# Round two of a graph propagation in 128 PSUM columns, and three steps moved off VectorE

## The chip, the cores and the metric
The kernel runs on one core of one Trainium2 chip. Its metric is the device time in microseconds (us) of one execution. A core has TensorE (matmuls; PE in the profile, its weight loads are the row PEld), VectorE (DVE), ScalarE (ACT), GpSimd (POOL) and SyncE (SP, which here issues all the transfers). Matmuls write into PSUM; the other memory, SBUF, has 128 partitions.

## What is computed
The input x has 4096 rows of 128 features, adj is a 4096 x 4096 matrix of zeros and ones. Cut to what matters:

```
xh   = layernorm(x)
U    = softmax over edges of leaky_relu(xh @ a1 + (xh @ a2).T)    # 4096 x 4096
feat = shrink(c1 * xh + U @ xh - rowsum * xh)
pu   = U @ feat
x1   = x + mix(feat, pu, h0, rowsum)
z, xBC, dt = split(layernorm(x1) @ W_in)                          # Mamba-2 block
xBC  = silu(causal conv of 4 taps (xBC)); xs, B, C = split(xBC)
dt   = softplus(dt + dt_bias); dA = dt * -exp(A_log)              # 4 heads
y    = within-chunk part (exp of segment sums of dA) + state part + D * xs
out  = x1 + rmsnorm(y * silu(z)) @ W_out @ W_lin + b_lin
```

U is never built. exp(leaky_relu(f1 + f2)) is one of two products of a row weight and a column weight, depending on the sign of f1 + f2. So each edge has a code, and from a block of codes two masks of zeros and ones are made: maskA for positive logits, maskC for the others. U times something is maskA times Y of side 0 plus maskC times Y of side 1, where Y holds the column-weighted features.

## The kernel before
The 4096 rows are 32 tiles of 128 (NT = 32). Masks are in fp32r, a type of 4 bytes that TensorE multiplies in one pass, where plain fp32 takes two instructions; Y keeps each feature as a high part (rounded to fp32r) and a low part (the rest), `Y[:, jt, side, part, :]`. A mask is the stationary operand of its matmul; the moving operand is both parts of Y side by side. In round one these are 2 x 130 columns (features and two extra columns), in round two 2 x 128 = 256. The result therefore stands in PSUM as two halves (high and low) which VectorE adds later.

Round one: adj is loaded, transposed on TensorE (L1223), coded by VectorE (L683) and stored to DRAM as int8 codes; masks of 128x1024 are made by ScalarE (maskA, L1053) and VectorE (maskC, L691); `products` (L1273) multiplies them. Between the rounds Y is made anew from feat, in four quarters of 8 column tiles (y_second, L670).

Round two runs in slots, one tile in each (`slot` in each engine's block, ordered by `schedule`, L235). In slot s TensorE works on the products of tile s, four blocks (block(0) to block(3)) of 8 maskA and 8 maskC matmuls, and between the blocks on the Mamba-2 steps of the tiles s-1 to s-4, one stage behind another (`ok[0]` to `ok[4]` say which exist). Five slots after the last products drain the stages. The order on each engine is written out by hand; engines wait for each other by semaphores only. Masks rotate through 4 buffers, so that a new mask waits for the matmuls of the block four before it.

What the change touches, with the lines of the kernel before:
- TensorE: L1283 and L1293 (products), L1421 (the segment sums: `after`, a triangular matrix of ones, times dam, 4 heads x 128), L1442 (B times C, which needs C on partitions 0 to 63, `cT`). Both rounds go through `products`; XC = 130 columns in round one, F = 128 in round two.
- VectorE: L845 (weighted sum of accC and the scaled accA, both halves at once, into `part`), L862 (adds the two halves), L867 (x1), L912 (`normalise2`, the second layernorm), L985 and L986 (last product of the convolution's silu into xbc; L986 does it again for C, to the lower partitions).
- ScalarE: L1072 (read_acc, scales accA), L1152 (xn2T, copy of the transposed tile, which releases L1386), L1160 to L1205.
- GpSimd: L562, L563 (rstd of the second layernorm), L573 (dam = upto times dA, 128x512), L581 to L592.
- dam and `after` are plain fp32. dA, 4 numbers for each partition, stands in `tiny`.

Of the kernel before, what the change touches and what calls it, by code (L numbers as in the profile page):

```python
# [36 lines left out]
def gnn_ffn_kernel(nc, x, adj, h0, a, temp, W_in, conv_w, conv_b, dt_bias, A_log, D, norm_w, W_out, W_lin, b_lin, out):  # L37
# [20 lines left out]
    with ExitStack() as ctx:  # L58
# [9 lines left out]
        adj_in = sb("adj_in", [P, 4, IT, JH * P])  # L68
        edges = sb("edges", [P, 4, IT, 2 * P], BF16)
        code = sb("code", [P, 2, IT, NT * P], I8)  # L70
# [54 lines left out]
        class Space:  # L125
# [43 lines left out]
        upto = rows_space.take(P)  # L169
        after = rows_space.take(P)  # L170

# [29 lines left out]
        junk = y_space.take(DI)  # L201
        sum2 = y_space.take(2 * F)
        tiny = rows_space.take(16, 8)
# [13 lines left out]
            mix_ready xdt_ready  ps_ready y_read yg_ready st_done skip_ready yT_ready ssq_ready rs_ready  # L217
            exp_done out_done zcopy""".split()
        S = {n: sem(n) for n in names}
# [156 lines left out]
        def _(pool):  # L376
# [179 lines left out]
            def slot(s_, k, now, then, ok):  # L556
                if ok[0]:

                    kt = (k - 1) % SLOTS
                    wait(pool, "ln_done", s_)  # L560
                    wait(pool, "xn2_ready", s_ - 1)
                    link(g.tensor_tensor(tiny[:, 1, 0:1], tiny[:, 0, 1:2], consts[:, 2, 0:1], ALU.add))  # L562
                    g.tensor_tensor(tiny[:, 1, 1:2], tiny[:, 1, 0:1], consts[:, 0, 0:1], ALU.pow).then_inc(S["rstd2"], 1)  # L563

                    wait(pool, "out_done", s_ - 4)
                    g.tensor_tensor(x1b[:, kt], x1[:, kt % 2], b_row, ALU.add).then_inc(S["x1b_done"], 1)
                if now:
                    base_of(s_, k)
                if ok[1]:

                    wait(pool, "dt_ready", s_ - 1)
                    wait(pool, "p_cum", s_ - 2)
                    g.tensor_tensor(dam, upto.unsqueeze(1).broadcast_to([P, NH, P]),  # L573
                                    tiny[:, 2 + k % 2, NH:2 * NH].unsqueeze(2).broadcast_to([P, NH, P]), ALU.mult).then_inc(S["dam_ready"], 1)
                if ok[2]:

                    kc = (k - 3) % 2
                    wait(pool, "xl_ready", s_ - 2)
                    wait(pool, "p_s", s_ - 3)
                    dtc = tiny[:, 2 + kc, 0:NH]  # L580
                    link(g.tensor_tensor(heads(xdt, HD), heads(xl[:, 0:DI], HD), dtc.unsqueeze(2).broadcast_to([P, NH, HD]), ALU.mult))  # L581
                    wait(pool, "exp_done", s_ - 2)
                    g.tensor_tensor(heads(xdtd, HD), heads(xdt, HD), expD[:, :, P - 1:P].broadcast_to([P, NH, HD]), ALU.mult).then_inc(S["xdt_ready"], 1)
                    wait(pool, "st_done", s_ - 3)
                    g.tensor_tensor(heads(pstate[0:DS], HD), heads(state[0:DS, kc], HD),
                                    tiny[0:DS, 4 + kc, NH:2 * NH].unsqueeze(2).broadcast_to([DS, NH, HD]), ALU.mult).then_inc(S["ps_ready"], 1)
                if ok[3]:

                    wait(pool, "ssq_ready", s_ - 3)
                    wait(pool, "out_done", s_ - 4)  # L590
                    link(g.tensor_tensor(tiny[:, 6, 0:1], tiny[:, 6, 1:2], consts[:, 3, 0:1], ALU.add))
                    g.tensor_tensor(tiny[:, 6, 2:3], tiny[:, 6, 0:1], consts[:, 0, 0:1], ALU.pow).then_inc(S["rs_ready"], 1)  # L592
                end_chain()
# [6 lines left out]
        def _(dve):  # L600
# [223 lines left out]
            def slot(s_, k, now, then, ok):  # L824
# [6 lines left out]
                kt = (k - 1) % 2  # L831
                part = sum2.rearrange("p (a b) -> p a b", a=2)
                if ok[4]:
# [29 lines left out]
                if ok[0]:  # L863

                    dve.wait_ge(S["vch"], halves)
                    wait(dve, "x1b_done", T - 1)
                    v.scalar_tensor_tensor(out=x1[:, kt], in0=part[:, 0], scalar=row_out[:, bass.ds(row, 1), 0:1].rearrange("p a b -> p (a b)"), in1=base[:, kt],  # L867
                                           op0=ALU.mult, op1=ALU.add).then_inc(S["x1_done"], 1)
# [38 lines left out]
                def normalise2():  # L907

                    if ok[0]:
                        dve.wait_ge(S["rstd2"], s_)  # L910
                        wait(dve, "p_xT", s_ - 2)
                        v.tensor_scalar(xn2[:, kt], x1[:, kt], tiny[:, 0, 0:1], tiny[:, 1, 1:2], ALU.subtract, ALU.mult).then_inc(S["xn2_ready"], 1)  # L912

# [18 lines left out]
                if ok[1]:  # L932
# [25 lines left out]
                    last = step(v.tensor_tensor(p, horner[:, 2, :, 5], si, ALU.mult))  # L958
                    normalise2()
                    y_state()  # L960
# [7 lines left out]
                else:  # L968
                    normalise2()
                    y_state()  # L970
# [7 lines left out]
                if ok[1]:  # L978
# [5 lines left out]
                    wait(dve, "p_y", s_ - 3)  # L984
                    v.scalar_tensor_tensor(out=xbc[:, k2], in0=gate_t, scalar=1.0, in1=conv, op0=ALU.add, op1=ALU.mult)  # L985
                    v.scalar_tensor_tensor(out=cT[0:DS, k2], in0=gate_t[DS:P, CB - 1], scalar=1.0, in1=conv[DS:P, CB - 1], op0=ALU.add,  # L986
                                           op1=ALU.mult).then_inc(S["conv_ready"], 1)
                mask(3)
# [6 lines left out]
        def _(act):  # L995
# [66 lines left out]
            def read_acc(T, k, cols, round_two=0):  # L1062
# [7 lines left out]
                w = roww[:, bass.ds(row, 1), 0:1].rearrange("p a b -> p (a b)")  # L1070
                src = accA[k][:, 0:2 * cols].rearrange("p (a b) -> p a b", a=2)
                s.mul(acc_s[:, k, :, 0:cols], src, w).then_inc(S["acc_read"], 1)  # L1072

# [66 lines left out]
            def slot(s_, k, now, then, ok):  # L1140
# [71 lines left out]
        def _(pe):  # L1212
# [60 lines left out]
            def products(n, k, b, ch, cols, y=None, between=None):  # L1273
# [78 lines left out]
            def slot(s_, k, now, then, ok):  # L1352
# [57 lines left out]
                if ok[2]:  # L1410
# [66 lines left out]
```

## Time and profile before

| | us |
|---|---|
| three runs | 901.5, 902.1, 906.4 (median 902.1) |
| the profiled execution | 900.56 |
| its span, first to last instruction | 898.8 |
| TensorE, weight loads, VectorE, ScalarE, GpSimd busy | 818.9, 767.0, 792.5, 592.0, 543.9 |
| mean granted TensorE clock | 0.957 of 2.4 GHz |

Round one takes the first 400 us, the change of Y lasts to about 430, and slots with all stages run from about 470 to 855. A busy time is the union of an engine's instructions; matmuls overlap, so their pace is read from one start to the next, not from their duration. A clock of 1.00 is 2.4 GHz, 0.50 is 1.2 GHz.

### The profile page before, as it was taken

The page shows a single profiled execution, that of the slowest core. Times are in us where ns is not written, and L with a number is a line of the kernel's source. Part 1 is how long each engine was busy: PE and PEld are TensorE (multiplying, and loading weights), DVE is VectorE, ACT ScalarE, POOL GpSimd, SP SyncE. Part 2 cuts the span into 40 slices and gives each one's busy share as a digit, 9 for nine tenths or more (in the row PEclk, how much of TensorE's full clock was granted, in tenths as well). Part 3 has the DMA queues.
Part 4 walks back from the last instruction along what each step waited for, and adds up shares of the span by engine and source line. Part 5 has one row for each costly group of instructions (what it writes and reads, how often), then busy time and mean ns, then how long its engine had stood idle before and what let it go on. Part 6 is the DMA issues. An engine that isn't in the chain of part 4 may idle for free.

```text
span 898.8 us, 21768 instructions
## 1 busy us (share of the span) xinstructions
PE 818.9 (91%) x6650; PEld 767.0 (85%) x6650; DVE 792.5 (88%) x1968; ACT 592.0 (66%) x1026; POOL 543.9 (61%) x1123
## 2 busy tenths in 40 slices
PE   3978999989998999955889999999999999999976
PEld 1668999989998999954889999999999999999954
DVE  6567999989998999657699999999999999999983
ACT  6676877778787887533566666666666666666641
POOL 4462556664655666788656666575665756666642
PEclk9878999999999999995899999999999999999997
DMA  6456978878696967700111112111121111110000
GB/s 190 141 187 196 286 254 267 266 215 280 206 306 195 308 206 258 224 3 24 36 60 62 50 50 66 36 61 58 38 64 35 61 58 41 61 36 16 7 7 10
DMA packets 97545, 110.72 MB, mean 123 GB/s; under 512 B 6464, under 2 KB 89280, under 8 KB 97472
## 3 DMA queue, kind: packets, MB, share of 16 engines
q1 hardware_dynamic: 97472, 109.74, 38.7%
q8 instruction: 46, 0.75, 0.4%
q14 instruction: 27, 0.22, 0.1%
HBM read 90.85 MB, written 18.87 MB: 122 GB/s over the span
## 4 chain that ended last, share of the span: by engine, by line
PE 40%; POOL 20%; issue 13%; DVE 12%; ACT 8%; DMA 5%; POOLq 1%; DVEq 1%; ACTq 0%; SPq 0%
PE accA L1283 12%; PE accC L1293 11%; DMA adj_in<-in_adj_dram 5%; ACT edges L1006 3%; PE ps L1223 3%; PE ps L1421 2%; DVE maskC L691 2%; PE ps L1401 2%; PE ps L1399 2%; ACT maskA L1053 2%; DVE code L683 2%; POOL small L471 2%; DVE code L895 1%; PE ps L1403 1%; POOL featsum L490 1%
## 5 line engine op out<-in xcount | busy, mean ns | idle before, releaser
L1283 PE MATMUL accA<-Y,maskA 128*128 128x260 f32 (+1 forms) x2048 | 313.8, 296 | 30.5 <-DVE Y L662 19.1
L1053 ACT ACTIVATE maskA<-code 128x1024 fp32r<-128x1024 int8 x256 | 269.3, 1053 | 56.6 <-PE accC L1293 28.3
L1283 PEld LDWEIGHTS accA<-Y,maskA 128*128 128x128 f32 x2048 | 270.0, 193 | 33.7 <-ACT maskA L1053 16.9
L1293 PE MATMUL accC<-Y,maskC 128*128 128x260 f32 (+1 forms) x2048 | 295.3, 288 | 1.1 <-DVE maskC L691 1.1
L1293 PEld LDWEIGHTS accC<-Y,maskC 128*128 128x128 f32 x2048 | 268.4, 194 | 1.4 <-DVE maskC L691 1.4
L683 DVE SCALAR_TENSOR_TENSOR code<-f_rows,neg_f,ps 128x512 int8<-128x512 f32 x256 | 178.4, 740 | 37.1 <-PE ps L1223 35.5
L691 DVE TENSOR_SCALAR maskC<-code 128x1024 fp32r<-128x1024 int8 x256 | 210.0, 824 | 1.2 <-issue 0.3
L1006 ACT ACTIVATE edges<-adj_in 128x1024 bf16<-128x1024 f32 x128 | 133.1, 1044 | 24.5 <-DMA adj_in<-in_adj_dram 16.4
L895 DVE SCALAR_TENSOR_TENSOR code<-adj_in,f_rows,code 128x128 f32<-128x128 f32 x288 | 113.7, 415 | 0.0
L1223 PE MATMUL ps<-ident,edges 128*128 128x128 bf16 x1024 | 82.5, 225 | 13.3 <-ACT edges L1006 9.8
L1223 PEld LDWEIGHTS ps<-ident,edges 128*128 128x128 bf16 x1024 | 60.7, 101 | 24.1 <-DVE code L683 8.0
L562 POOL TENSOR_TENSOR f_rows<-f_rows,consts 128x1 f32<-128x1 f32 x32 | 8.4, 263 | 118.6 <-DVE f_rows L905 118.6
L573 POOL TENSOR_TENSOR f_rows<-f_rows 128x512 f32<-128x512 f32 x32 | 39.1, 1220 | 31.6 <-DVE f_rows L967 30.4
L462 POOL COPY small<-roww 128x2 f32 (+1 forms) x32 | 6.3, 198 | 83.2 <-DVE ps_sum L709 81.4
L1201 ACT COPY adj_in<-ps 128x256 f32<-128x256 f32 x32 | 12.0, 375 | 49.6 <-PE ps L1433 49.6
L1160 ACT COPY code<-ps 128x260 f32<-128x260 f32 x32 | 12.0, 376 | 48.7 <-PE ps L1388 48.7
L1183 ACT ACTIVATE code<-code 128x384 f32<-128x384 f32 x32 | 16.8, 525 | 35.6 <-DVE code L895 35.6
L1165 ACT ACTIVATE code<-ps,f_rows 128x128 f32<-128x128 f32 x96 | 37.5, 474 | 0.0
L581 POOL TENSOR_TENSOR adj_in<-code,f_rows 128x256 f32<-128x256 f32 x32 | 32.2, 1006 | 7.2 <-ACT code L1190 7.2
L1401 PE MATMUL ps<-adj_in,code 128*128 128x64 f32 x256 | 36.5, 266 | 0.0
L1421 PE MATMUL ps<-f_rows 128*128 128x512 f32 x64 | 36.0, 646 | 0.0
L1399 PE MATMUL ps<-adj_in,code 128*128 128x128 f32 x128 | 30.0, 317 | 6.2 <-DVE code L852 5.4
(201 smaller groups left out, 1487.3 us busy)
## 6 DMA issues: line engine op xcount, KB each, us to landing
adj_in<-in_adj_dram SPq DMA_DIRECT2D x128, 512.0 KB, 4.6
edge_codes<-code SPq DMA_DIRECT2D x8, 2048.0 KB, 10.0
code<-edge_codes SPq DMA_DIRECT2D x32, 512.0 KB, 3.3
xn<-in_x_dram SPq DMA_DIRECT2D x4, 512.0 KB, 5.8
adj_in<-in_x_dram SPq DMA_DIRECT2D x32, 64.0 KB, 1.8
adj_in<-in_L_gnn_h_dram SPq DMA_DIRECT2D x32, 64.0 KB, 1.9
out_dram<-adj_in SPq DMA_DIRECT2D x32, 64.0 KB, 1.6
f_rows<-in_L_ffn_W_in_dram SPq DMA_DIRECT2D x1, 192.0 KB, 6.6
```

The source lines that it names most:

```text
L573: g.tensor_tensor(dam, upto.unsqueeze(1).broadcast_to([P, NH, P]), tiny[:, 2 + k % 2, NH:2 * NH].unsqueeze(2).broadcast_to([P, NH, P]), AL ...
L683: v.scalar_tensor_tensor(out=code[:, par, :, jt * P:(jt + 1) * P], in0=f1_rows[:, rows].rearrange("p (i r) -> p i r", i=IT), scalar=neg_f2 ...
L691: v.tensor_scalar(maskC[:, b % MASKS], src, 2.0, None, ALU.is_equal).then_inc(S["maskC_ready"], 1)
L895: ins = v.scalar_tensor_tensor(out=conv[:, cb], in0=hist[:, k2, cb, tap:tap + P], scalar=conv_wt[:, cb, tap:tap + 1], in1=conv[:, cb], op0 ...
L1006: s.activation(edges[:, h % 4], adj_in[:, h % 4], ACT.Sign).then_inc(S["signed"], 1)
L1053: s.activation(maskA[:, b % MASKS], src, ACT.Relu, bias=-2.0).then_inc(S["maskA_ready"], 1)
L1223: m = t_.matmul(ps[jt % TRB][:, it * P:(it + 1) * P], edges[:, b % 4, it, j * P:(j + 1) * P], ident2[:], start=True, stop=True)
L1283: t_.matmul(accA[k][:, 0:2 * cols], maskA[:, b % MASKS, l * P:(l + 1) * P], Y[:, jt, 0, :, 0:cols], start=jt == 0, stop=jt == NT - 1)
L1293: m = t_.matmul(accC[k][:, 0:2 * cols], maskC[:, b % MASKS, l * P:(l + 1) * P], Y[:, jt, 1, :, 0:cols], start=jt == 0, stop=jt == NT - 1)
L1399: t_.matmul(ps[0][:, kb * P:(kb + 1) * P], xbc[:, (k - 4) % 2, kb, :], skip_w[:, kb], start=True, stop=False)
L1401: t_.matmul(ps[0][:, h * HD:(h + 1) * HD], wmix[:, h], xdt[:, h * HD:(h + 1) * HD], start=False, stop=h == (kb + 1) * P // HD - 1)
L1421: t_.matmul(ps[3][:, 0:NH * P], after, dam.rearrange("p h w -> p (h w)"), start=True, stop=True)
```

## The change
Four things, in one edit:
1. In round two each mask is multiplied twice, by the high part and by the low part of Y, 128 columns each, both accumulating into the same 128 columns of PSUM. L845 and read_acc work on 128 columns, L862 goes. Round one stays as it is.
2. dA is split into an fp32r high part and a rest (`da_parts`, two small products on GpSimd), dam is made for both (128x1024, fp32r), and L1421 becomes two fp32r matmuls that accumulate. dam, `after` and da_parts lie where `edges` lay in round one.
3. The normalisation L912 goes to ScalarE, as an activation with scale rstd and bias -mean * rstd; GpSimd makes that bias.
4. L986 goes. ScalarE copies C from xbc to `cT` at the start of the next slot, ahead of xn2T, under a new semaphore cT_ready, for which L1442 waits.

```diff
-        dam = rows_space.take(NH, P)
+        dam = edge_space.take(2, NH, P)
+        after = edge_space.take(P)
+        da_parts = edge_space.take(2, NH)
...
-                    g.tensor_tensor(tiny[:, 1, 1:2], tiny[:, 1, 0:1], consts[:, 0, 0:1], ALU.pow).then_inc(S["rstd2"], 1)
+                    link(g.tensor_tensor(tiny[:, 1, 1:2], tiny[:, 1, 0:1], consts[:, 0, 0:1], ALU.pow))
+                    g.tensor_scalar(tiny[:, 1, 2:3], tiny[:, 0, 0:1], tiny[:, 1, 1:2], -1.0, ALU.mult, ALU.mult).then_inc(S["rstd2"], 1)
...
-                    g.tensor_tensor(dam, upto.unsqueeze(1).broadcast_to([P, NH, P]),
-                                    tiny[:, 2 + k % 2, NH:2 * NH].unsqueeze(2).broadcast_to([P, NH, P]), ALU.mult).then_inc(S["dam_ready"], 1)
+                    da = tiny[:, 2 + k % 2, NH:2 * NH]
+                    link(g.tensor_tensor(da_parts[:, 0], tiny[:, 2 + k % 2, 0:NH], a_row, ALU.mult))
+                    link(g.tensor_tensor(da_parts[:, 1], da, da_parts[:, 0].bitcast(F32), ALU.subtract))
+                    g.tensor_tensor(dam.rearrange("p a h w -> p (a h) w"), upto.unsqueeze(1).broadcast_to([P, 2 * NH, P]),
+                                    da_parts.rearrange("p a h -> p (a h)").bitcast(F32).unsqueeze(2).broadcast_to([P, 2 * NH, P]),
+                                    ALU.mult).then_inc(S["dam_ready"], 1)
...
                     halves = step(v.scalar_tensor_tensor(
-                        out=part, in0=accC[kt][:, 0:2 * F].rearrange("p (a b) -> p a b", a=2),
-                        scalar=roww[:, bass.ds(row, 1), 1:2].rearrange("p a b -> p (a b)"), in1=acc_s[:, kt, :, 0:F], op0=ALU.mult, op1=ALU.add))
+                        out=sum2, in0=accC[kt][:, 0:F],
+                        scalar=roww[:, bass.ds(row, 1), 1:2].rearrange("p a b -> p (a b)"), in1=acc_s[:, kt, 0, 0:F], op0=ALU.mult, op1=ALU.add))
...
-                    halves = step(v.tensor_tensor(part[:, 0], part[:, 0], part[:, 1], ALU.add))
...
-                        v.tensor_scalar(xn2[:, kt], x1[:, kt], tiny[:, 0, 0:1], tiny[:, 1, 1:2], ALU.subtract, ALU.mult).then_inc(S["xn2_ready"], 1)
...
+                    wait(dve, "cT_ready", s_ - 3)
+                    v.scalar_tensor_tensor(out=xbc[:, k2], in0=gate_t, scalar=1.0, in1=conv, op0=ALU.add, op1=ALU.mult).then_inc(S["conv_ready"], 1)
...
+                if round_two:
+                    s.mul(acc_s[:, k, 0, 0:F], accA[k][:, 0:F], w).then_inc(S["acc_read"], 1)
...
+                if ok[2]:
+                    act.wait_ge(S["conv_ready"], s_ - 2)
+                    wait(act, "p_y", s_ - 4)
+                    s.copy(cT[0:DS, (k - 3) % 2], xbc[DS:P, (k - 3) % 2, CB - 1]).then_inc(S["cT_ready"], 1)
...
                 mask(2)
+                if ok[0]:
+                    act.wait_ge(S["rstd2"], s_)
+                    wait(act, "p_xT", s_ - 2)
+                    s.activation(xn2[:, (k - 1) % 2], x1[:, (k - 1) % 2], ACT.Identity, bias=tiny[:, 1, 2:3], scale=tiny[:, 1, 1:2]).then_inc(S["xn2_ready"], 1)
...
+                    if cols == F:
+                        for part in range(2):
+                            t_.matmul(accA[k][:, 0:F], maskA[:, b % MASKS, l * P:(l + 1) * P], Y[:, jt, 0, part, 0:F],
+                                      start=jt == 0 and part == 0, stop=jt == NT - 1 and part == 1)
...
-                    t_.matmul(ps[3][:, 0:NH * P], after, dam.rearrange("p h w -> p (h w)"), start=True, stop=True)
+                    for half in range(2):
+                        t_.matmul(ps[3][:, 0:NH * P], after, dam[:, half].rearrange("p h w -> p (h w)"), start=half == 0, stop=half == 1)
...
+                    pe.wait_ge(S["cT_ready"], s_ - 2)
```

## Rows read from the trace of the kernel before

**Rows 1.** The page, part 1: busy time, share of the span, instructions.

```profile
PE 818.9 (91%) x6650; PEld 767.0 (85%) x6650; DVE 792.5 (88%) x1968; ACT 592.0 (66%) x1026; POOL 543.9 (61%) x1123
```

**Rows 2.** Stretches: length, busy us (instructions) of PE, PEld, DVE, ACT, POOL, clock, DMA.

```profile
460.00:860.00 400.00, 395.92 (x3022) 371.45 (x3021) 392.05 (x1116) 258.85 (x602) 253.19 (x430) 1.00 0.15 47
634.69:648.61 13.92, 13.87 (x108) 12.98 (x107) 13.62 (x40) 9.09 (x21) 8.60 (x16) 1.00 0.16 52
```

**Rows 3.** Waits from 460 to 860 us: who waited for whom, total, times, longest.

```profile
PEld ps L1399 <- DVE code L852: 7.7, 21, 2.2
```

**Rows 4.** Groups by shape, whole span: count, busy us, mean ns, idle before.

```profile
L1283 PEld LDWEIGHTS accA<-Y,maskA 128*128 128x128 f32 x2048 | 270.0, 193 | 33.7 <-ACT maskA L1053 16.9 <-ACT acc_s L1072 8.6 <-issue 6.6
...
L1283 PE MATMUL accA<-Y,maskA 128*128 128x256 f32 x1024 | 158.6, 298 | 19.1 <-DVE Y L662 19.1
```

**Rows 5.** TensorE in order of time, one slot: start us, length us, group.

```profile
636.34 0.56 PE L1401 MATMUL ps<-adj_in,code 128*128 128x64 f32 x4
636.73 0.44 PE L1399 MATMUL ps<-adj_in,code 128*128 128x128 f32 x2
...
638.84 1.12 PE L1293 MATMUL accC<-Y,maskC 128*128 128x256 f32 x8
639.80 0.59 PE L1409 MATMUL ps<-f_rows,code 128*128 128x256 f32 x2
...
640.59 1.11 PE L1421 MATMUL ps<-f_rows 128*128 128x512 f32 x2
641.54 0.49 PE L1423 MATMUL ps<-ident,code 128*128 128x128 f32 x3
...
646.13 0.61 PE L1448 MATMUL ps<-f_rows,adj_in 128*128 128x128 f32 x4
646.58 0.27 PE L1377 MATMUL ps<-ident,adj_in 128*128 128x128 f32 x1
```

**Rows 6.** TensorE in order of time, the matmuls of one column and what follows.

```profile
41.33 3.63 PE L1260 MATMUL accA<-a_col,code 128*128 128x1 f32 x32
44.82 2.63 PE L1326 MATMUL accC<-xn,ones 128*128 128x128 f32 x16
```

**Rows 7.** Line L1326: its weight loads, shortest, median and longest in ns.

```profile
L1326 PEld LDWEIGHTS accC<-xn,ones x64: 190/192/338, 44.8 to 76.1; 128*128 128x128 f32 x64
```

**Rows 8.** Four stretches, columns as in rows 2 (the clock comes behind POOL).

```profile
41.30:44.80 3.50, 3.50 (x33) 3.47 (x32) 1.81 (x2) 0.70 (x2) 0.13 (x1) 1.00 0.24 85
46.10:49.50 3.40, 3.40 (x29) 3.28 (x28) 1.59 (x3) 2.35 (x4) 2.70 (x2) 0.50 0.49 144
...
419.00:434.00 15.00, 10.05 (x42) 9.23 (x43) 9.51 (x16) 5.06 (x7) 12.16 (x32) 0.50 0.11 37
434.00:440.00 6.00, 6.00 (x47) 6.00 (x47) 2.91 (x8) 4.00 (x4) 2.75 (x7) 0.90 0.18 38
```

**Rows 9.** TensorE in order of time, the last quarter of tile 0.

```profile
429.72 2.05 PE L1283 MATMUL accA<-Y,maskA 128*128 128x256 f32 x8 [2.71 <-DVE Y L662]
431.57 1.91 PE L1293 MATMUL accC<-Y,maskC 128*128 128x256 f32 x8
```

**Rows 10.** TensorE in order of time near the end, at the low clock.

```profile
879.90 0.95 PE L1401 MATMUL ps<-adj_in,code 128*128 128x64 f32 x4
880.65 0.74 PE L1399 MATMUL ps<-adj_in,code 128*128 128x128 f32 x2
```

**Rows 11.** Groups by shape, 460 to 860 us: VectorE, ScalarE, GpSimd.

```profile
L1165 ACT ACTIVATE code<-ps,f_rows 128x128 f32<-128x128 f32 x87 | 34.0, 474 | 0.0
...
L573 POOL TENSOR_TENSOR f_rows<-f_rows 128x512 f32<-128x512 f32 x29 | 35.3, 1216 | 22.0 <-DVE f_rows L967 21.0 <-PE ps L1423 1.0
...
L986 DVE SCALAR_TENSOR_TENSOR f_rows<-code 64x128 f32<-64x128 f32 x29 | 17.7, 609 | 0.4
L912 DVE TENSOR_SCALAR adj_in<-adj_in,f_rows 128x128 f32<-128x128 f32 x29 | 14.2, 489 | 0.0
```

**Rows 12.** TensorE in order of time in round one: bf16 transposes.

```profile
205.02 0.62 PE L1223 MATMUL ps<-ident,edges 128*128 128x128 bf16 x8
```

More of the change, by code:

```diff
@@ L68, in gnn_ffn_kernel @@
         adj_in = sb("adj_in", [P, 4, IT, JH * P])
-        edges = sb("edges", [P, 4, IT, 2 * P], BF16)
+        with nc.sbuf_tensor("edges", [P, 4, IT, 2 * P], BF16) as edges:
+            pass
+        edge_room = sb("edge_room", [P, 4 * IT * P], F32R)
         code = sb("code", [P, 2, IT, NT * P], I8)
@@ L146, in gnn_ffn_kernel @@
         y_space = Space(ywork[:, :])
+        edge_space = Space(edge_room[:, :])
         DI = W_out.shape[0]
@@ L169, in gnn_ffn_kernel @@
         upto = rows_space.take(P)
-        after = rows_space.take(P)
         x_in = adj_space.take(2, F)
@@ L201, in gnn_ffn_kernel @@
         junk = y_space.take(DI)
-        sum2 = y_space.take(2 * F)
+        sum2 = y_space.take(F)
         tiny = rows_space.take(16, 8)
@@ L217, in gnn_ffn_kernel @@
             mix_ready xdt_ready  ps_ready y_read yg_ready st_done skip_ready yT_ready ssq_ready rs_ready
-            exp_done out_done zcopy""".split()
+            exp_done out_done zcopy cT_ready""".split()
         S = {n: sem(n) for n in names}
@@ L831, in slot @@
                 kt = (k - 1) % 2
-                part = sum2.rearrange("p (a b) -> p a b", a=2)
                 if ok[4]:
@@ L861, in slot @@
                     dve.wait_ge(S["vch"], halves)
-                    halves = step(v.tensor_tensor(part[:, 0], part[:, 0], part[:, 1], ALU.add))
-                if ok[0]:
-                    dve.wait_ge(S["vch"], halves)
                     wait(dve, "x1b_done", T - 1)
-                    v.scalar_tensor_tensor(out=x1[:, kt], in0=part[:, 0], scalar=row_out[:, bass.ds(row, 1), 0:1].rearrange("p a b -> p (a b)"), in1=base[:, kt],
+                    v.scalar_tensor_tensor(out=x1[:, kt], in0=sum2, scalar=row_out[:, bass.ds(row, 1), 0:1].rearrange("p a b -> p (a b)"), in1=base[:, kt],
                                            op0=ALU.mult, op1=ALU.add).then_inc(S["x1_done"], 1)
@@ L968, in slot @@
                 else:
-                    normalise2()
                     y_state()
@@ L984, in slot @@
                     wait(dve, "p_y", s_ - 3)
-                    v.scalar_tensor_tensor(out=xbc[:, k2], in0=gate_t, scalar=1.0, in1=conv, op0=ALU.add, op1=ALU.mult)
-                    v.scalar_tensor_tensor(out=cT[0:DS, k2], in0=gate_t[DS:P, CB - 1], scalar=1.0, in1=conv[DS:P, CB - 1], op0=ALU.add,
-                                           op1=ALU.mult).then_inc(S["conv_ready"], 1)
+                    wait(dve, "cT_ready", s_ - 3)
+                    v.scalar_tensor_tensor(out=xbc[:, k2], in0=gate_t, scalar=1.0, in1=conv, op0=ALU.add, op1=ALU.mult).then_inc(S["conv_ready"], 1)
                 mask(3)
@@ L1070, in read_acc @@
                 w = roww[:, bass.ds(row, 1), 0:1].rearrange("p a b -> p (a b)")
-                src = accA[k][:, 0:2 * cols].rearrange("p (a b) -> p a b", a=2)
-                s.mul(acc_s[:, k, :, 0:cols], src, w).then_inc(S["acc_read"], 1)
+                if round_two:
+                    s.mul(acc_s[:, k, 0, 0:F], accA[k][:, 0:F], w).then_inc(S["acc_read"], 1)
+                else:
+                    src = accA[k][:, 0:2 * cols].rearrange("p (a b) -> p a b", a=2)
+                    s.mul(acc_s[:, k, :, 0:cols], src, w).then_inc(S["acc_read"], 1)
             def supertile(G, par, first=False, last=False):
@@ L1282, in products @@
                     jt = ch * JB + l
-                    t_.matmul(accA[k][:, 0:2 * cols], maskA[:, b % MASKS, l * P:(l + 1) * P], Y[:, jt, 0, :, 0:cols],
-                              start=jt == 0, stop=jt == NT - 1)
+                    if cols == F:
+                        for part in range(2):
+                            t_.matmul(accA[k][:, 0:F], maskA[:, b % MASKS, l * P:(l + 1) * P], Y[:, jt, 0, part, 0:F],
+                                      start=jt == 0 and part == 0, stop=jt == NT - 1 and part == 1)
+                    else:
+                        t_.matmul(accA[k][:, 0:2 * cols], maskA[:, b % MASKS, l * P:(l + 1) * P], Y[:, jt, 0, :, 0:cols],
+                                  start=jt == 0, stop=jt == NT - 1)
                 if between is not None:
@@ L1292, in products @@
                     jt = ch * JB + l
-                    m = t_.matmul(accC[k][:, 0:2 * cols], maskC[:, b % MASKS, l * P:(l + 1) * P], Y[:, jt, 1, :, 0:cols],
-                                  start=jt == 0, stop=jt == NT - 1)
+                    if cols == F:
+                        for part in range(2):
+                            m = t_.matmul(accC[k][:, 0:F], maskC[:, b % MASKS, l * P:(l + 1) * P], Y[:, jt, 1, part, 0:F],
+                                          start=jt == 0 and part == 0, stop=jt == NT - 1 and part == 1)
+                    else:
+                        m = t_.matmul(accC[k][:, 0:2 * cols], maskC[:, b % MASKS, l * P:(l + 1) * P], Y[:, jt, 1, :, 0:cols],
+                                      start=jt == 0, stop=jt == NT - 1)
                 m.then_inc(S["mm_done"], 1)
```

5 lines of the change are left out of this document (removed).

## Prediction
> **What bounds the kernel now.** I read the page's first two parts, then busy time in chosen stretches, then the waits of round two, then TensorE in order of time. The page gives TensorE 91% and VectorE 88% of the span [rows 1]; such an average can't say which is late, so I cut out round two. From 460 to 860 us TensorE is busy 395.9 of 400 us and VectorE 392.1; in one slot (634.69 to 648.61, 13.92 us) they are busy 13.87 and 13.62, with ScalarE at 9.09 and GpSimd at 8.60, all at a granted clock of 1.00 [rows 2]. The waits settle the order: of TensorE's waits the longest is for the product L852 of VectorE, 7.7 us in 21 of 29 slots, read on its weight loads [rows 3]; VectorE has none of a microsecond or two. So a slot is TensorE's queue, back to back, with VectorE just behind it. Taking work off VectorE alone gives back those 7.7 us at most; adding work to TensorE costs its full time.
>
> **The part that decides: two matmuls a mask.** A tile multiplies 32 masks of each kind, 64 in all. Round two now has 1024 matmuls of 256 columns on each of L1283 and L1293 [rows 4]. Eight take 0.96 us (638.84 to 639.80): 120 ns each [rows 5]. After the change each mask has two of 128 columns. By columns alone two halves cost what one whole did, so the question is what one matmul costs however short it is. Every matmul in the trace has its own weight load: TensorE and its load row both count 6650 [rows 1]. L1260 shows the floor: 32 matmuls of one column, 41.33 to 44.82 us, are 109 ns apiece although they stream nothing; L1448 (128 columns of plain fp32) takes 0.45 us for 4, 112 ns [rows 6, 5]. L1326's loads, from plain fp32, last 192 ns, and those of the masks, fp32r, 193 [rows 7, 4]: they look like the same load, of which one fits in about 112 ns. So a matmul of 128 columns costs 112 ns, set by the load, and a mask 2 x 112 = 224 ns in place of 120: 104 ns more. 64 x 104 ns = 6.66 us a tile. Tiles 1 to 31 lie on the full queue: 31 x 6.66 = +206 us. The bounds: below, 97 ns (L1401, 64 columns, 0.39 us for 4 [rows 5]), 194 a mask, +147 us; above, the 120 ns that the present pair takes, 240 a mask, +238 us. I take 112, the row with the same 128 columns.
>
> The Trainium skill (TensorE: Matmul & The Clock Gate, LDWEIGHTS) has a load last its columns over 1.2 GHz, 107 ns for 128, whatever the array's clock; the rows agree at the high level and not at the low one, below. By 107 ns that term would be 64 x 94 ns x 31 = +186 us.
>
> **The same at the low clock.** From 419 to 434 us the clock is at 0.50, that is 1.2 GHz [rows 8]. Eight of the present matmuls take 1.85 us there, 231 ns each [rows 9]; L1401, 64 columns, takes 0.75 us for 4, 188 ns, against 97 at the high level [rows 10, 5]. So the load slows with the clock, and a mask of two matmuls costs 376 to 462 ns there: take 400. Tile 0 runs at the low level but waits for Y between its quarters (2.71 us before the last [rows 9]), which hides most of its extra time; about 3 us of its last quarter don't hide. The clock rises now from 434 us on, while the last quarter and tile 1 stream without a pause [rows 8]. In halves the array streams only about half the time, so it may rise later: one more tile at the low level is 64 x (400 - 224) ns = 11 us. It may be none or three; I take +14 us for start and last quarter together.
>
> **Split dam.** TensorE now makes L1421 as plain fp32, two instructions over 512 columns, 0.95 us (640.59 to 641.54) [rows 5]. As two fp32r matmuls of 512 columns it costs at most twice a 256-column one each, 4 x 120 ns = 0.48 us: -0.47 us a slot, 31 slots on the full queue, -15 us. (Zero gain is the other bound, if fp32r were no faster there.) GpSimd pays: L573 (128x512, 1.22 us) doubles, two small products and the negated product for ScalarE come to it at 0.2 to 0.3 us each [rows 11]: +2 us on 8.6 of a slot of 13.9, hidden; the dam made in one slot is wanted by L1421 of the next, which starts 13.9 us after 640.6.
>
> **Work off VectorE.** L912 goes (0.49), L986 goes (0.61) [rows 11], and with them the sum L862 and half of L845, two short ones: some -1.5 us a slot on VectorE. TensorE was the bound, so this is worth only its waits for L852, which with a longer slot vanish: -8 us. Waits elsewhere are already nil.
>
> **Work and waits on ScalarE.** The normalisation is an activation with scale and bias like L1165, 0.47 us [rows 11]; the copy of C to the lower partitions, 64x128, is at most that; read_acc halves. Under +1 us on 9.1: hidden. The copy waits for conv_ready, and behind it on ScalarE stands xn2T, which releases L1386. By the slot's order conv is complete near the end of VectorE's slot and xn2T is wanted by L1386 only after the first block, 1.9 us into TensorE's; after the change that block lasts 32 x 112 = 3.6 us. The normalisation waits for a third small GpSimd step after L563 (ends 639.83); it would stand behind mask 2, before TensorE's next slot needs it at 646.6 (L1377). Without that cover the two cost 0.3 us a slot, 9 us; 0 is taken. VectorE, at 12.3 us in a slot of 20, has room.
>
> **Sum.** +206 + 14 - 15 - 8 = +197 us. The profiled execution took 900.6 us (span 898.8): 1097. The median is 1.5 us higher: **1099 us**. A slot goes from 13.9 to about 20 us. With the pace's bounds and the clock's start the forecast's own range is 1040 to 1150.
>
> **The rivals.**
> *A, the second half is free.* The mask doesn't change between the two halves; if its load is left out the second time, or an fp32r load takes as long as a bf16 one, two halves cost 2 x 56 = 112 ns (L1223, 128 columns of bf16: 8 last 0.62 us with the 0.2 us tail of the last, so about 56 apiece [rows 12]), no more than now. Then the slot is TensorE's old queue without 0.47 us, with VectorE well off it: 902 - 15 - 5 (most of the waits for L852) = 882 us. It decides from 65 ns a half down: 2 x 65 - 120 = 10 ns, times 64 x 31, is the 20 us that the rest brings. For it: no matmul of this trace repeats single-pass weights, so a left-out load could not have shown. Against: the fp32r load's 193 ns, and L1326, which multiplies eight times running by the same ones and has 64 loads for 64 matmuls [rows 7] (in two passes of fp32, so no proof). This one ends faster than before. Between this and the forecast lies a load that overlaps in part. The rows of fp32 loads are all at or above 97 ns, so that gets little.
>
> The Trainium skill (TensorE: Matmul & The Clock Gate, Back-to-back issue gap) gives about 81 ns for a 128-column load-and-matmul pair in a stream; by that figure a mask costs 162 ns, the term is +83 us and the time about 975 us. No fp32 row here comes as low.
>
> *B, a short fp32r matmul goes at the fp32 pace.* No fp32r matmul under 256 columns is in the trace. If a half took two passes, it costs 224 ns and a mask 448: 64 x 328 ns x 31 = +651 us, about 1530.
>
> *C, the clock doesn't hold.* During L1260 loads follow one another without a gap and the array streams one column each; the clock, 1.00 in that stretch, is 0.50 from 46.1 to 49.5 us [rows 8]. Loads alone don't hold it. In halves the array streams 128 columns (53 ns at 2.4 GHz) in each 112. If that isn't enough, a slot has 64 x 400 ns = 25.6 us of masks, and the rest (13.9 - 7.7 - 0.5 = 5.7 us) doubles to 11.4: 37 us, 23 more than now, 1615 us if always, about 1230 if the low level takes a quarter of the slots beyond the forecast's. For it: the stretch behind L1260. Against: a slot has over 5 us of full streaming beside the masks, and in round two the clock fell once only, near 470, after a wait for L852. Whether half is enough no row here shows.
>
> The Trainium skill (TensorE: Matmul & The Clock Gate, What's actually happening) has the gate follow how busy the array has been; the stretch behind L1260 agrees.
>
> **How the numbers follow.** Forecast 0.69; A 0.11, of it 0.09 with the half free and the rest with the overlap in part; B 0.07; C 0.12, half of it under 1300; else 0.01. The range reaches from 1020 to 1300: that holds the forecast and half of C, about 0.75 to 0.8. Under 0.5% of 902, some 4.5 us, a difference can't be told from none. Faster 0.09, within 0.5% 0.01, slower 0.90.
>
> **What would show it.** TensorE's matmuls and loads go from 6650 to 8698 (+2048; L1421 stays at 64). If loads are fewer, A. Sixteen of a block's halves after one another should take 1.8 us; 0.96 us means A, 3.5 us B or C, and the granted clock of 500 to 1000 us tells these two apart: 1.00 for B. L1421's two should take 0.43 to 0.48 us. VectorE should wait, for matmuls that free its mask buffers, some 7 us a slot, and its busy share in round two fall from 98% to about 62%; TensorE's wait for L852 should be gone. Round one should be unchanged. The forecast is wrong if the slot is under 17 or over 22 us.

## The result: 1106.9 us, 22% slower, and the profile after

| | before | after |
|---|---|---|
| median of the runs, us | 903.7 (five runs) | 1106.9 (five runs) |
| ratio, 95% interval | | 1.224 (1.219 to 1.229) |
| span of the profiled execution | 898.8 | 1122.7 |
| TensorE, VectorE, GpSimd busy | 818.9, 792.5, 543.9 | 1055.4, 706.0, 603.0 |

The profiled execution of after is a slow one, the longest of the five at 1124.4 us with a mean granted clock of 0.924, where the other four took 1104.6 to 1107.4 us at 0.936 to 0.942; the ratio leaves it out. The forecast was 1099 us.

The page of after, part 1, and two of its groups by shape (behind the bar: busy us, mean ns of one, idle us before), beside [rows 1, 4]:

```profile
PE 1055.4 (94%) x8698; PEld 1021.0 (91%) x8698; DVE 706.0 (63%) x1872; ACT 622.7 (55%) x1090; POOL 603.0 (54%) x1219
...
L1292 PEld LDWEIGHTS accA<-Y,maskA 128*128 128x128 f32 x2048 | 262.6, 206 | 13.4 <-ACT acc_s L1070 8.7 <-ACT maskA L1048 3.3
...
L1439 PE MATMUL ps<-edge_room 128*128 128x512 f32 x64 | 22.8, 437 | 0.0
```

There are 8698 matmuls and as many loads: nothing was left out for the mask that doesn't change. One slot of after on TensorE in order of time, beside [rows 5]:

```profile
699.83 0.27 PE L1394 MATMUL ps<-ident,adj_in 128*128 128x128 f32 x1
699.86 1.98 PE L1292 MATMUL accA<-Y,maskA 128*128 128x128 f32 x16
701.68 1.95 PE L1307 MATMUL accC<-Y,maskC 128*128 128x128 f32 x16
703.46 0.65 PE L1403 MATMUL ps<-f_rows,adj_in 128*128 128x260 f32 x2
...
710.76 0.71 PE L1439 MATMUL ps<-edge_room 128*128 128x512 f32 x2
711.31 0.49 PE L1441 MATMUL ps<-ident,code 128*128 128x128 f32 x3
...
719.65 0.27 PE L1394 MATMUL ps<-ident,adj_in 128*128 128x128 f32 x1
```

Sixteen halves take 1.78 us (701.68 to 703.46): 111 ns each, 222 a mask, where the one matmul of 256 columns took 120. The slot lasts 19.82 us (699.83 to 719.65) against 13.92. The pair L1439 (710.76 to 711.31) takes 0.55 us against L1421's 0.95. Stretches of after, columns as in [rows 2]: one slot, the last quarter of tile 0 and what follows up to 509 us, and all slots behind:

```profile
699.83:719.65 19.82, 19.82 (x173) 19.52 (x171) 10.95 (x36) 10.11 (x24) 10.70 (x18) 1.00 0.11 36
419.00:434.00 15.00, 14.36 (x67) 14.06 (x66) 11.70 (x21) 5.18 (x6) 12.01 (x21) 0.50 0.11 37
434.00:509.00 75.00, 72.80 (x338) 72.28 (x338) 18.97 (x50) 17.33 (x29) 19.47 (x46) 0.50 0.06 20
...
520.00:1040.00 520.00, 520.00 (x4464) 512.15 (x4463) 287.21 (x943) 264.45 (x602) 280.58 (x472) 1.00 0.11 35
```

TensorE is busy without a gap and VectorE only 55% (287 of 520). The clock, which before rose at about 434 us [rows 8], is at 0.50 until 509 us, and from then on at 1.00 for the rest of the full slots. What a half costs at the low level is seen in tile 1 (TensorE in order of time):

```profile
443.21 3.62 PE L1292 MATMUL accA<-Y,maskA 128*128 128x128 f32 x16
446.63 3.62 PE L1307 MATMUL accC<-Y,maskC 128*128 128x128 f32 x16
```

3.42 us for 16: 214 ns each, nearly twice the 111 ns at the full clock. And who waits in the full slots of after (who for whom, total us, times, longest):

```profile
POOL f_rows L566 <- DVE f_rows L910: 206.4, 26, 8.1
DVE adj_in L846 <- PE ps L1467: 141.0, 26, 5.5
ACT adj_in L1208 <- PE ps L1451: 117.1, 26, 4.5
```

TensorE isn't in the list; its waits for L852 [rows 3] are gone. Where the 223.9 us between the two profiled spans lie, by the starts of the slots: up to the end of tile 3 58.8 us (it is done at 521.4 in place of 462.6), the next slot 2.3, 27 full slots 160.0 (5.93 each), the end 2.8.

### The profile page after: what moved, and what is told of

Its sections match the earlier page's. It is cut to its first block, busy times and chain, and to the rows that moved or that the text cites. A ratio compares the mean times of both kernels' runs of the same rounds, so it can differ in the third digit from the quotient of the medians.

```text
span 1122.7 us, 25954 instructions
## 1 busy us (share of the span) xinstructions
PE 1055.4 (94%) x8698; PEld 1021.0 (91%) x8698; DVE 706.0 (63%) x1872; ACT 622.7 (55%) x1090; POOL 603.0 (54%) x1219
## 4 chain that ended last, share of the span: by engine, by line
PE 70%; POOL 10%; ACT 6%; issue 5%; DVE 4%; DMA 4%; POOLq 0%; DVEq 0%; ACTq 0%; SPq 0%
PE accC L1307 21%; PE accA L1292 21%; DMA adj_in<-in_adj_dram 4%; PE accA L1295 4%; PE accC L1310 3%; ACT edges L1001 3%; PE ps L1418 2%; PE ps L1230 2%; PE ps L1405 2%; PE ps L1403 2%; PE ps L1439 2%; PE ps L1416 1%; PE ps L1467 1%; PE ps L1420 1%; PE ps L1426 1%
## 5 line engine op out<-in xcount | busy, mean ns | idle before, releaser
L1292 PE MATMUL accA<-Y,maskA 128*128 128x128 f32 x2048 | 277.3, 292 | 11.3 <-DVE Y L671 11.3
L1292 PEld LDWEIGHTS accA<-Y,maskA 128*128 128x128 f32 x2048 | 262.6, 206 | 13.4 <-ACT acc_s L1070 8.7
L1307 PE MATMUL accC<-Y,maskC 128*128 128x128 f32 x2048 | 272.3, 290 | 0.0
L1307 PEld LDWEIGHTS accC<-Y,maskC 128*128 128x128 f32 x2048 | 260.6, 206 | 0.0
L700 DVE TENSOR_SCALAR maskC<-code 128x1024 fp32r<-128x1024 int8 x256 | 192.5, 755 | 10.6 <-PE accC L1307 10.3
L1295 PE MATMUL accA<-Y,maskA 128*128 128x260 f32 x1024 | 158.0, 298 | 12.8 <-issue 7.6
L1310 PE MATMUL accC<-Y,maskC 128*128 128x260 f32 x1024 | 147.1, 287 | 1.1 <-DVE maskC L700 1.1
L1295 PEld LDWEIGHTS accA<-Y,maskA 128*128 128x128 f32 x1024 | 135.5, 195 | 13.4 <-issue 7.9
L1310 PEld LDWEIGHTS accC<-Y,maskC 128*128 128x128 f32 x1024 | 134.6, 194 | 1.5 <-DVE maskC L700 1.5
L846 DVE TENSOR_TENSOR adj_in<-ps,f_rows 128x128 f32<-128x128 f32 x32 | 9.3, 292 | 161.6 <-PE ps L1467 158.3
L900 DVE SCALAR_TENSOR_TENSOR code<-adj_in,f_rows,code 128x128 f32<-128x128 f32 x288 | 91.6, 338 | 0.0
L890 DVE TENSOR_TENSOR f_rows<-code,f_rows 128x4 f32<-128x4 f32 x32 | 5.2, 163 | 116.3 <-ACT code L1168 116.3
L581 POOL TENSOR_TENSOR edge_room<-f_rows,edge_room 128x1024 fp32r<-128x1024 f32 x32 | 61.5, 1923 | 2.5
```

Source lines behind the costliest of these rows:

```text
L581: g.tensor_tensor(dam.rearrange("p a h w -> p (a h) w"), upto.unsqueeze(1).broadcast_to([P, 2 * NH, P]), da_parts.rearrange("p a h -> p (a ...
L700: v.tensor_scalar(maskC[:, b % MASKS], src, 2.0, None, ALU.is_equal).then_inc(S["maskC_ready"], 1)
L900: ins = v.scalar_tensor_tensor(out=conv[:, cb], in0=hist[:, k2, cb, tap:tap + P], scalar=conv_wt[:, cb, tap:tap + 1], in1=conv[:, cb], op0 ...
L1292: t_.matmul(accA[k][:, 0:F], maskA[:, b % MASKS, l * P:(l + 1) * P], Y[:, jt, 0, part, 0:F], start=jt == 0 and part == 0, stop=jt == NT - ...
L1307: m = t_.matmul(accC[k][:, 0:F], maskC[:, b % MASKS, l * P:(l + 1) * P], Y[:, jt, 1, part, 0:F], start=jt == 0 and part == 0, stop=jt == N ...
```

## The experiments

All ratios are to runs of the kernel before on the same chip, with 95% intervals.

**1. One part alone: only the halves.**
```diff
-  t_.matmul(accA[k][:, 0:2 * cols], maskA[...], Y[:, jt, 0, :, 0:cols], ...)
+  for part in range(2):
+      t_.matmul(accA[k][:, 0:F], maskA[...], Y[:, jt, 0, part, 0:F], ...)
```


> The kernel before with only the two matmuls of 128 columns a mask in round two (and the 128-column sums that go with them). Theory (the weight load sets the pace, 112 ns a matmul): TensorE's slot is 13.9 + 64 x 104 ns = 20.6 us less the waits for L852, about 20.3 us; 8698 matmuls and loads (L1421 as before), time about 1120 us, some 15 us above the changed kernel. Rival (part of the loss comes from the steps moved to ScalarE and GpSimd or from the split dam): under 1080 us.

1121.3 us, ratio 1.238 (1.229 to 1.246). The slots are 20.2 us apart. The halves alone make the whole loss, and the other three steps, beside them, give back 0.4 us a slot. That is 12 to 14 us: 14 between the two medians, 12 when each is set against its own runs of before. TensorE has no wait for the product L852 in this trace either.

In its trace the clock rises late too, between 480 and 485 us:

```profile
434.00:480.00 46.00, 43.81 (x205) 43.54 (x205) 12.57 (x24) 9.85 (x12) 13.24 (x34) 0.50 0.06 18
485.00:500.00 15.00, 15.00 (x135) 14.94 (x135) 9.15 (x26) 6.51 (x13) 4.95 (x9) 1.00 0.14 45
```

**2. The rest alone: 256 columns a mask again.** The edit is the reverse of the one above, in the changed kernel.

> The changed kernel with one matmul of 256 columns a mask again; split dam, copy of C and normalisation on ScalarE stay. Theory: L1421 shorter by 0.4 us a slot and the waits for L852 gone: slot 13.3 to 13.5 us, about 883 us, 2% faster than before. Rival (the moved steps put a wait of 0.3 us or more a slot on xn2T or dam): 895 to 905 us.

939.0 us, ratio 1.036 (1.031 to 1.041): a miss of theory and rival. Three steps that I had held for gains or for hidden cost 33 us when TensorE's queue is short. The longest waits on three engines from 500 to 860 us, and the path in order of time (L601 is GpSimd's last step of a slot; it makes the row scale `rs_ready`, for which VectorE's L867 waits):

```profile
POOL f_rows L566 <- DVE f_rows L914: 59.3, 24, 2.7
DVE adj_in L867 <- POOL f_rows L601: 43.7, 24, 2.0
PEld ps L1407 <- issue: 29.9, 20, 1.6
```
```profile
640.93 0.18 DVE L914 BATCH_NORM_AGGREGATE f_rows<-f_rows 128x2 f32<-128x6 f32 x1
...
641.18 0.28 POOL L566 TENSOR_TENSOR f_rows<-f_rows,consts 128x1 f32<-128x1 f32 x1 [2.48 <-DVE f_rows L914]
...
648.50 1.91 POOL L581 TENSOR_TENSOR edge_room<-f_rows,edge_room 128x1024 fp32r<-128x1024 f32 x1
...
653.25 0.55 POOL L601 TENSOR_TENSOR f_rows<-f_rows,consts 128x1 f32<-128x1 f32 x1
...
653.94 0.35 DVE L867 SCALAR_TENSOR_TENSOR adj_in<-ps,f_rows,adj_in 128x128 f32<-128x128 f32 x1 [1.96 <-POOL f_rows L601]
...
656.14 0.17 DVE L914 BATCH_NORM_AGGREGATE f_rows<-f_rows 128x2 f32<-128x6 f32 x1
```

GpSimd waits for VectorE at the head of its slot and VectorE waits for GpSimd at the end of it: a ring. GpSimd works from 641.18 to 653.80 without a real gap, VectorE needs another 2.4 us up to the end of L914, and the slot is the sum, 15.2 us here. GpSimd's idle time in the slot was no slack: it was the other half of the ring.

**3. Only dam split.** The edit is the dam lines of the diff, in the kernel before.

> The kernel before with only dam split and L1421 in two fp32r matmuls. Theory: TensorE's slot falls by 0.4 us, but VectorE is busy 13.6 of 13.9 us, so it takes over the bound at once: 895 to 900 us. Rival (TensorE alone bounds the slot): 890 us or less. Other rival (GpSimd's 2 us more are late): over 902 us.

922.8 us, ratio 1.018 (1.014 to 1.023): the second rival. In the profile TensorE's wait in front of L1407 (for VectorE's product, L852 in the kernel before) is 1.0 us in each of 25 slots, and the slots are 14.3 to 14.8 us apart. So dam alone costs 16 us. The ring isn't what shows here: VectorE waits for GpSimd only 2.6 us in 15 slots and is busy 352 of 360 us. It is VectorE's own work that has become longer, beside GpSimd's doubled dam (L580):

```profile
641.85 1.97 POOL L580 TENSOR_TENSOR edge_room<-f_rows,edge_room 128x1024 fp32r<-128x1024 f32 x1
641.97 2.27 DVE L993 SCALAR_TENSOR_TENSOR code<-code 128x384 f32<-128x384 f32 x1
```

L993 is the same instruction as L985 in the kernel before, where it takes 0.97 us; here it begins just after GpSimd's product and ends 0.4 us after it, in nearly every slot (median 2.26 us), and so it does in experiments 8 and 9. When the dam product doesn't run beside it, as in the changed kernel, it takes 0.55 us.

**4. Halves from tile 4 on.** Tiles 0 to 3 keep 256 columns a mask.
```diff
+  narrow = not isinstance(s_, int) or s_ >= 4      # the tile's slot
-  if cols == F:
+  if narrow:
```


> The changed kernel, but tiles 0 to 3 of round two with one matmul of 256 columns a mask; halves from tile 4 on. Theory (halves keep TensorE's clock from rising but don't make it fall): the clock rises at about 434 us as in the kernel before and stays at 1.00 through the halves; time = 1106 - 4 x 6.7 us (fewer loads) - some 40 to 50 us of the low clock's cost = 1030 to 1040 us. Rival (the late rise costs nothing beyond the tiles' own price): about 1080 us. Other rival (halves let the clock fall whenever they start): granted clock 0.50 again after tile 4, 1100 us or more.

1081.9 us, ratio 1.197 (1.189 to 1.205). The runs are wide apart, 1069.3 to 1089.4, and the two shortest alone give 1.18; the profiled one is the fastest:

```profile
437.80:1031.00 593.20, 587.64 (x5012) 577.23 (x5011) 339.55 (x1103) 306.88 (x699) 324.80 (x551) 1.00 0.11 34
```

The clock rises at 437.8 us and, in this execution, holds through 28 tiles in halves: they don't make it fall. The other three executions have a lower mean clock (0.941 to 0.953 against 0.961), and where it was low in them isn't on record.

Tile 3 is done at 465.6 us, 55.8 earlier than in the profile of after (521.4). Three tiles' price at the high clock is 20 us, so some 36 us of that profile were the low clock: 6 before tile 1 starts, 13 in tile 1, 14 in tile 2, 3 in tile 3. In the trace of experiment 1 tile 3 is done at 510.9 us, and the same sum gives 26 us. For the other four runs of after, 18 us shorter than the profiled one, I estimate 18. The expectation of 1030 to 1040 us was missed, because its 40 to 50 us for the low clock was read off nothing better than the longest run. By the medians even the rival's number, 1080, came: 25 us lie between 1106.9 and 1081.9, and the tiles' own price is 20 to 27 of them. So that the low clock costs something is shown by the traces, and not by these medians.

**5. One load a mask, 128 columns** (the low part of Y is left out).
```diff
-  for part in range(2):
+  for part in range(1):
```


> The changed kernel, round two multiplies each mask by the high part of Y only: one matmul of 128 columns a mask (the low part is left out). Theory: one load a mask, 112 ns; TensorE's queue is 19.8 - 64 x 0.112 = 12.7 us a slot, so the ring through GpSimd (its steps of a slot, then VectorE's steps up to the mean and variance, then GpSimd again; about 15 us in the kernel with split dam and 256 columns) sets the slot: 14.9 to 15.2 us, about 940 us. Rival (TensorE is the only bound): 865 us. Other rival (a 128-column fp32r matmul has a slow mode of its own): matmul spacing over 120 ns.

981.2 us (two runs), ratio 1.084 (1.077 to 1.091). Eight matmuls take 0.90 us (L1307, 642.65 to 643.55): 112 ns with one load a mask as with two, so a matmul of 128 columns has no slow mode. The slots are 14.6 us apart where the clock is up, a little less than in experiment 2, and VectorE waits for GpSimd as there (35.9 us in 19 slots). The expected 940 us was missed by 41, and what I had left out is the clock:

```profile
609.00:720.00 111.00, 99.52 (x815) 95.58 (x813) 94.41 (x266) 74.98 (x179) 87.84 (x136) 1.00 0.15 49
721.00:745.00 24.00, 24.00 (x108) 23.15 (x107) 12.59 (x43) 10.09 (x23) 10.71 (x18) 0.50 0.10 33
```

TensorE waited some 11 of 111 us, its matmuls being short besides; then the clock was at 0.50 for 24 us. Such a stretch comes six times in round two, and a slot with one takes 22 us or more.

**6. Two loads a mask, 64 columns each** (half of the features and the low part are left out).
```diff
-  t_.matmul(accA[k][:, 0:F],  ..., Y[:, jt, 0, part, 0:F], ...)
+  t_.matmul(accA[k][:, 0:64], ..., Y[:, jt, 0, 0, part * 64:part * 64 + 64], ...)
```


> The changed kernel, but the two matmuls a mask have 64 columns each (64 features of the high part each, into the same 64 columns; the rest is left out): the array streams half as much as in the changed kernel, the loads are as many. Theory (load sets the pace): spacing 112 ns, slot 19.8 us, same time as the changed kernel, 1105 us, if the clock stays up. Rival (columns set the pace): slot about 16 us, 985 us. Clock: if streaming a quarter of the time doesn't hold it, the granted clock is 0.50 in most of round two and the time over 1300 us; I give that one in three.

1495.7 us (two runs). TensorE in order of time, and two stretches with their clocks:

```profile
698.35 3.60 PE L1292 MATMUL accA<-Y,maskA 128*128 128x64 f32 x16
701.76 3.60 PE L1307 MATMUL accC<-Y,maskC 128*128 128x64 f32 x16
710.52 2.27 PE L1292 MATMUL accA<-Y,maskA 128*128 128x64 f32 x16
712.62 2.01 PE L1307 MATMUL accC<-Y,maskC 128*128 128x64 f32 x16
```
```profile
698.30:705.00 6.70, 6.70 (x34) 6.70 (x32) 3.17 (x8) 1.32 (x2) 0.00 (x0) 0.50 0.03 10
711.00:714.00 3.00, 3.00 (x30) 3.00 (x28) 2.66 (x11) 2.48 (x5) 2.75 (x7) 1.00 0.47 143
577.00:1400.00 823.00, 823.00 (x4253) 806.70 (x4253) 276.94 (x904) 252.47 (x576) 255.50 (x451) 0.58 0.07 21
```

Half the columns and yet 3.41 us for 16 at the low clock, 213 ns each, exactly the 128-column price; at the high level it is 1.83 us (712.62 to 714.45), 114 ns each. So the columns don't set the pace. That a matmul costs as much with 64 columns of work and that the clock is low (0.58 over the slots) make this the dearest version, with no more arithmetic than experiment 5: the prediction's rival C, in a kernel one step further. I had given it one in three. TensorE had no pause in these 823 us, so here the clock fell without one.

**7. Copy of C and normalisation on ScalarE, nothing else.**

> The kernel before with only copy of C and second normalisation on ScalarE (256 columns a mask, dam as before). GpSimd gets 0.5 us more a slot, inside the 1.3 us that it had to spare before L858 needed it. Theory (ring through GpSimd): it fits, VectorE is off the bound, TensorE's wait for L852 goes: slot 13.7 us, 895 us. Rival (the copy or the normalisation on ScalarE is late for TensorE): over 905 us.

902.6 us, ratio 0.996 (0.994 to 0.998), a gain of 4 us where I expected 10. The slots start 13.6 us apart and go to 14.0; VectorE waits 1.3 us a slot for rs_ready (33.1 us in 26). So with VectorE relieved it is the ring that sets the slot: taking 1.5 us off VectorE and putting 0.5 on GpSimd leaves it at 14.0 us. This also says where experiment 2's loss lies. Dam alone costs 16 us and these two steps alone gain 4, but together they cost 33: in this ring the split of dam is worth 1.1 us a slot (14.0 to 15.1), not the 0.65 of experiment 3.

**8. Less work on GpSimd** (256 columns; of the base of x1, the weights of h0 and of the feature are left out).

> The changed kernel with 256 columns a mask again (the 939 us version), and GpSimd's four steps L546 to L549 that make up the base of x1 replaced by one addition (weights of h0 and of the feature left out): some 1.8 us less GpSimd work a slot. Theory (the ring through GpSimd set 15.0 us a slot): slot falls to TensorE's own 13.5 us, about 890 us. Rival (contention between GpSimd's fp32r writes and VectorE, or the waits on ScalarE, set it): stays above 925 us.

905.0 us, ratio 1.001 (0.999 to 1.003): 32 to 34 us better than experiment 2, but not the 890 of the theory. The slots are 14.0 us. There is a second ring, over dt_ready:

```profile
POOL edge_room L576 <- DVE f_rows L965: 18.4, 26, 0.8
DVE adj_in L864 <- POOL f_rows L598: 14.5, 26, 1.9
```

VectorE makes dA (L965), and GpSimd works from L576 (700.40 us) to the end of L598 (707.39) on dam, xdt and rs_ready. VectorE goes on with L864 at 707.53 and is at the next dA at 714.13. The two parts make up the slot. This ring is read from the waits; no edit here tried it by itself.

**9. The same work, another order.** GpSimd's base of x1 goes to the head of its slot, where it waits anyway; 256 columns, split dam.
```diff
 def slot(s_, k, now, then, ok):          # GpSimd
+    if now:
+        base_of(s_, k)
     if ok[0]:
         wait(pool, "ln_done", s_)
...
-    if now:
-        base_of(s_, k)
```


> The changed kernel with 256 columns a mask (939 us), GpSimd's base of x1 (L546 to L554, 3.1 us) moved from behind its step on the variance to the head of its slot, where it waits for VectorE anyway; all work as before. Theory (the ring GpSimd, rs_ready, L867, x1, ln_done, GpSimd sets 15.0 us): the ring loses 3.1 us, what is left is the ring through dam (from dt_ready over dam and xdt to rs_ready and back, 14.0 us as in the run with less GpSimd work): about 905 us. Rival (GpSimd's and VectorE's operations slow each other down, whatever the order): stays above 930 us.

911.7 us, ratio 1.010 (1.007 to 1.014): 27 us for nothing but order, or 24 when each kernel is set against its own runs of before. VectorE's wait for rs_ready fell from 43.7 to 12.6 us. So the ring was the cause of most of experiment 2's 33 us. Had it been that GpSimd and VectorE slow each other down, the order wouldn't have helped. The slots of 14.2 us fit the second ring: GpSimd waits for VectorE's dA (L968), 37.8 us in 23 slots.

**10. Experiment 7 with the base first.**

> Copy of C and normalisation on ScalarE, dam as before, 256 columns a mask (902.6 us), base first on GpSimd. Theory: VectorE's wait of 1.3 us a slot for rs_ready goes, the slot falls from 14.0 to TensorE's own 13.6 us: 890 us. Rival (contention of VectorE and GpSimd sets the slot): 900 us or more.

893.6 us, ratio 0.988 (0.985 to 0.992). Slots of 13.6 us, TensorE busy 330.0 of 330 us from 500 on: TensorE bounds again.

**11. Halves with bf16 masks and bf16 Y** (kernel of experiment 1).
```diff
-  maskA = sb("maskA", [P, MASKS, JB * P], F32R)      # maskC and Y likewise
+  maskA = sb("maskA", [P, MASKS, JB * P], BF16)
```


> The kernel before with halves only (1121 us), masks and Y in bf16 in both rounds (the high part of Y rounded to bf16, the low part the rest in bf16). Theory (the load of a 4-byte mask sets 112 ns): a bf16 load is short, spacing 56 ns, 112 ns a mask: TensorE's slot 13.2 us, so VectorE bounds at 13.4 to 13.6 us; about 890 us, and the clock rises at about 440 us. Rival (a matmul of 128 columns costs 112 ns whatever the mask's type): 1110 us.

883.4 us, ratio 0.978 (0.974 to 0.982), against 1121.3 with the same instructions on 4-byte masks. TensorE in order of time, and the start of round two as a stretch:

```profile
702.57 1.06 PE L1284 MATMUL accA<-Y,maskA 128*128 128x128 bf16 x16
703.46 1.07 PE L1299 MATMUL accC<-Y,maskC 128*128 128x128 bf16 x16
704.37 0.65 PE L1418 MATMUL ps<-f_rows,code 128*128 128x256 f32 x2
```
```profile
425.00:500.00 75.00, 72.30 (x981) 68.03 (x980) 68.08 (x194) 49.67 (x109) 45.24 (x81) 1.00 0.19 59
```

0.90 us for 16, 56 ns each; the load lasts 98 ns instead of 206. The clock is up from 425 us. The edit isn't confined to round two: tile 1 is done at 431.9 us, where it is done at 441.8 in the kernel before, so about 10 of the 18 us between the two spans lie ahead of it. Y in two bf16 parts is also coarser than in two fp32r parts, so this is not quite the same arithmetic.

**12. All that helped:** bf16, halves, copy and normalisation on ScalarE, base first, dam whole.

> bf16 masks and Y, two matmuls of 128 columns a mask, copy of C and normalisation on ScalarE, base first on GpSimd, dam as before. Theory: TensorE 13.1 us a slot, VectorE 12.3, the ring through dam 12.8: slot 13.1 to 13.3 us, 870 to 880 us. Rival (VectorE and GpSimd slow each other down further): 890 us or more.

880.1 us, ratio 0.973 (0.970 to 0.976), the lowest median, though its interval overlaps that of experiment 11. Slots of 13.3 us, TensorE busy 330.0 of 330 us.

## Why the prediction was right, and where not

*Two matmuls a mask.* Right. Predicted 224 ns a mask and +6.66 us a tile; measured 222 and, with the other parts, +5.93 a slot where the parts summed to 6.66 - 0.47 - 0.26 = 5.93. That they agree to the last digit is luck: the halves came out 0.08 us a slot cheaper (20.21 - 13.89 = 6.32 in experiment 1, against 6.66 - 0.26) and dam 0.07 dearer. Experiments 5 and 6 (128 or 64 columns, one matmul a mask or two) show that it isn't the columns, and 11 (as many instructions, 2-byte operands) that it goes with the type, as the load's length does: 98 ns against 206. Every matmul here has its own load, and experiment 11 changed mask and Y together; so the load can't be told from another fixed cost of a 4-byte matmul, and that it is the load is the reading that fits, not shown by itself.

*The low clock.* The mechanism was right, the size low: I took 400 ns a mask and one tile, +14 us with tile 0's part. It is 427 ns, and the term comes to 36 us in the profiled execution, 26 in that of experiment 1, and an estimated 18 in the other runs of after. In the profiled execution it was more than two tiles, and tile 0 hid less than I took: tile 1 starts at 443.2 us, against 433.3 before and 436.9 in experiment 4. Rival C, the clock that doesn't hold, didn't come: 1.00 from 509 us on. Experiments 5 and 6 show how near it lay.

*Split dam.* L1439 takes 0.55 us, not 0.48: -0.40 us a slot instead of -0.47. Over 31 slots that is 12 us for the predicted 15, as experiment 1 bears out (12 to 14). The waits for L852, the -8 us, aren't in this difference: they are gone with the halves alone too.

*"Hidden" on GpSimd and ScalarE.* Right for the changed kernel, and for GpSimd for the wrong reason. I set its 2 us against the idle part of a slot of 13.9 us. With TensorE's queue that short, the moved steps cost 1.2 us a slot, 33 us in all (experiment 2). The step that failed is taking an engine's idle share for slack: GpSimd's wait in a slot was for VectorE, and VectorE's next step waited for GpSimd. And GpSimd's longer product made VectorE's instruction beside it longer (experiment 3). In the changed kernel the slot of 19.8 us is longer than the ring of 15, and that is what hides it. ScalarE's two steps, for which I had named 0.3 us a slot, cost nothing even with a short queue (experiment 10: TensorE without a pause). Rival A's figure was wrong too: with the second half free, the kernel as written would have taken about 939 us by experiment 2 (an estimate), not 882.

*Rivals and signs.* A: all 8698 loads are there, and the fp32r load isn't short; it is short in bf16. B: no slow mode at 128 columns. One sign was read wrongly: VectorE is busy 55% and not 62%, and it waits for TensorE's last product of a slot (L846, 5.4 us a slot) and for ScalarE (L890, 3.4), not for its mask buffers.

## What to carry to other kernels

Price a matmul by the longer of its stream and its weight load, and read the load's pace from matmuls with next to no columns; a split of the moving operand is free only while each piece is longer than the load. Masks of zeros and ones lose nothing in 2 bytes; what they are multiplied by may. Before work is put on an idle engine, follow what it waits for: if that engine waits in turn for its result, the ring's sum counts, and moving independent work into the wait is the cure.

## What the hardware showed that I had not expected

- A matmul with a 4-byte load goes at 111 to 114 ns at 2.4 GHz and at 213 at 1.2, for 64 and 128 columns of work alike (experiments 5 and 6, tile 1 of after). The Trainium skill (TensorE: Matmul & The Clock Gate, LDWEIGHTS) has 107 ns without regard to the clock; at the low level the measurement decides.
- The clock stayed at 0.50 from 434 to 509 us while TensorE was 97% busy (72.8 of 75 us) with halves, and rose just behind the Mamba-2 steps of tile 3's first block (507 to 509 us). In experiment 1 it rose at about 484 us, some 2 us behind the first such steps (479.7 to 481.8). In after the same first steps, at 477.5 to 479.6 us, brought no rise. So what brings it isn't shown; but a busy TensorE in the profile doesn't say that the clock will rise.
- A VectorE instruction of one shape took 0.55, 0.97 or 2.26 us, as it ran beside other work of GpSimd or not (experiment 3); that GpSimd is the cause is read from the times, not tried by itself. Busy times of one kernel are no constants for the next.
- VectorE's steps of the convolution took 415 ns each before and 338 after, for the same shape. It isn't GpSimd's load: in experiment 1, where GpSimd is busy only 148 of 350 us, they take 421. They are short in experiment 7, so the change goes with the two steps moved to ScalarE and the order that this gives; the cause stays open.
